# Softplus as exp and ln in small steps, and a new timetable for them, in a decoder layer on one core

## The reference, cut to what matters

```python
hidden = _rmsnorm(residual, norm_w)
x, z = jnp.split(hidden @ W_in, 2, axis=-1)          # 1024 channels each
x = silu(causal_conv(x, conv_w, 4 taps) + conv_b)
x_dbl = x @ W_x                                      # 64 + 16 + 16 columns
dt = jax.nn.softplus(x_dbl[..., :DT_RANK] @ W_dt + b_dt)
Bm, Cm = x_dbl[..., 64:80], x_dbl[..., 80:]
A = -jnp.exp(A_log)
def step(h, inp):                                    # over the 224 rows
    x_t, dt_t, B_t, C_t = inp
    dA = jnp.exp(dt_t[..., None] * A)
    h = dA * h + (dt_t * x_t)[..., None] * B_t[:, None, :]
    return h, jnp.einsum('bdn,bn->bd', h, C_t)
y = (scan(step) + x * D) * silu(z)
out = residual + y @ W_out
```

## Time and profile before

| | |
|---|---|
| median of 3 runs | 3411.76 us (3411.43 to 3412.63) |
| the profiled execution's own time | 3412.63 us |
| its span, first to last instruction | 3411.2 us |
| PE, DVE, ACT, POOL busy over the span | 92%, 75%, 66%, 51% |
| first scan to last scan of the first phase | 83 to 1867 us |
| ACT table loads in the program | 97, of 1283 ns each |

### The profile page before, as it was taken

The page is one execution under the profiler, slowest core; times in us unless marked ns, Lnnn a source line. Parts: engine busy times, 40 slices in busy tenths (PEclk is TensorE's granted clock), DMA queues, the critical chain, the costliest instruction groups (busy, mean ns, idle before and its releaser), DMA issues. The chain is left out here.

```text
span 3411.2 us, 59151 instructions
## 1 busy us (share of the span) xinstructions
PE 3150.7 (92%) x20736; PEld 2194.3 (64%) x20736; DVE 2573.8 (75%) x4542; ACT 2262.6 (66%) x5049; POOL 1741.6 (51%) x1195
## 2 busy tenths in 40 slices
PE   5699899999999989999998899999999999899999
PEld 4567566665666656665665566666666666578887
DVE  1899999999999999999977577777777777523232
ACT  4678777777778777777764577777777777622222
POOL 1677888788887888788885000100000000055554
PEclk8899999999999999999999899999999999999999
DMA  6667667676777667667665121211211221210100
GB/s 180 167 182 191 182 173 189 180 192 179 175 184 186 184 166 189 187 180 185 173 172 175 54 73 54 89 50 48 84 59 48 75 69 61 65 59 25 47 28 25
DMA packets 286293, 424.98 MB, mean 125 GB/s; under 512 B 28753, under 2 KB 226129, under 8 KB 281394
## 3 DMA queue, kind: packets, MB, share of 16 engines
q1 hardware_dynamic: 278637, 411.44, 44.0%
q10 hardware_dynamic: 7365, 9.77, 1.0%
HBM read 320.12 MB, written 101.02 MB: 123 GB/s over the span
## 5 line engine op out<-in xcount | busy, mean ns | idle before, releaser
L772 POOL TENSOR_TENSOR a_hs<-a_rep,a_bmat 128x896 f32<-128x896 f32 x512 | 1061.4, 2096 | 323.7 <-PE a_yps L319 321.5
L439 ACT ACTIVATE a_states<-a_rep,a_a_neg 128x224 f32<-128x224 f32 x2048 | 795.7, 439 | 205.7 <-DVE a_hs L675 198.0
L668 DVE TENSOR_TENSOR_SCAN a_states<-a_states,a_hs 128x900 f32<-128x900 f32 x384 | 778.9, 2028 | 97.4 <-ACT a_states L439 95.0
L1381 DVE CUSTOM_DVE_ANT_0 b_sc<-sps,early_mask 112x375 f32<-112x375 f32 x1024 | 499.6, 544 | 134.6 <-PE sps L1127 128.7
L1268 ACT ACTIVATE b_sc<-b_sc,b_nmax 112x750 f32<-112x750 f32 x512 | 467.2, 913 | 0.7 <-DVE b_nmax L1387 0.7
L1141 PEld LDWEIGHTS b_tps<-ident,b_sc 112*125 112x125 f32 x3072 | 358.1, 189 | 168.8 <-issue 118.4
L341 PE MATMUL a_work<-early_scan_hT,w_in 128*128 128x224 f32 x2048 | 433.3, 370 | 13.5 <-issue 9.8
L341 PEld LDWEIGHTS a_work<-early_scan_hT,w_in 128*128 128x128 f32 x2048 | 411.8, 202 | 39.4 <-issue 29.2
L1141 PE MATMUL b_tps<-ident,b_sc 112*125 112x112 f32 x3072 | 405.3, 281 | 26.0 <-DVE b_pT L1395 18.8
L675 DVE TENSOR_TENSOR a_hs<-a_states,a_cmat 128x896 f32<-128x896 f32 x384 | 419.0, 1091 | 13.2
L1521 POOL TENSOR_SCALAR b_x_var<-mv 112x2 f32<-112x2 f32 x16 | 3.4, 214 | 814.8 <-DVE mv L1432 814.8
(11 more groups left out here) (189 smaller groups left out, 4735.5 us busy)
## 6 DMA issues: line engine op xcount, KB each, us to landing
a_rep<-du_scratch SPq DMA_DIRECT2D x512, 224.0 KB, 5.5
w_in<-W_in_dram SPq DMA_DIRECT2D x128, 512.0 KB, 4.4
du_scratch<-early_du SPq DMA_DIRECT2D x16, 1792.0 KB, 6.3
ctx<-ctxT_dram SPq DMA_DIRECT2D x48, 500.0 KB, 5.8
v_scratch<-kv_out SPq DMA_DIRECT2D x96, 250.0 KB
k_scratch<-kv_out SPq DMA_DIRECT2D x96, 250.0 KB, 4.4
b_keys<-k_scratch SPq DMA_DIRECT2D x8, 1500.0 KB, 9.6
b_v<-v_scratch SPq DMA_DIRECT2D x8, 1500.0 KB
```

What stands on the lines that cost most here:

```text
L439: e = act.activation(rows(states[:, g % DA, :])[:, q, 1:ROW], rep[tile % REPS][:, j, 0, :], ACT.Exp, scale=a_neg[:, g % SLOTS, q:q + 1])
L668: dve.tensor_tensor_scan(state if g % G4 else whole, state, whole, 0.0, ALU.mult, ALU.add).then_inc(S["scan"], 1)
L772: pool.tensor_tensor(hs[g % RING][:, :, 1:ROW], rep[tile % REPS][:, j, 1, :].unsqueeze(1).broadcast_to([P, Q, L]), bmat[b % 2][:], ALU.mul ...
L1381: dve.tensor_tensor_reduce(out=sc[buffer_of(block)][:, j, cols], in0=sps[0:TT, j, 0:HALF], in1=mask[:, block % 2, cols], scale=-1.0, scala ...
```

## The change

Softplus is no longer one activation but max(x, 0) + ln(1 + exp(-|x|)), pair by pair. ScalarE (`softplus_parts`): Abs into the buffer "conv", Relu into "dt", Exp, and a Square with a bias, written back to the PSUM bank. VectorE (`softplus_series`): two operations on it that make the first terms of a series for small arguments, the second added into dt. ScalarE (`softplus_log`): Ln and a Relu with a bias, in "conv". GpSimd (`softplus_sum`): dt + conv for the whole batch, 128 x 1792, ahead of the product u. The bank is now free when VectorE's second operation is done. All functions are in the table set of the exponentials, so the loads around the softplus go (97 become 66). The next batch's last tap waits for the sum, since "conv" is in use until then.

The timetable changes with it. For `LATER`, in slots of the batch that is scanned: dt from 18, 18, 21, 21 to 6, 8, 10, 12; parts in 7, 9, 11, 13, series in 8, 10, 12, 14, logs in 9, 11, 13, 15, the sum in 18; silu of z from 25 to 20, u from 26 to 20, its store from 24 to 21, z one slot earlier. Three units of keys and values per batch move by a slot or two; in the last batch but one two move from slots 6 and 8, one from 29, to 18, 19 and 20.

```diff
-            "x_dbl": [-33], "xd": [-32], "store_bc": [-32], "dt": [-18, -18, -15, -15],
-            "softplus": [-15, -15, -15, -15], "skip": [-20, -19], "spread": [-19], "silu_z": [-11], "u": [-10],
+            "x_dbl": [-33], "xd": [-32], "store_bc": [-32], "dt": spaced(-30, 2), "parts": spaced(-29, 2),
+            "series": spaced(-28, 2), "logs": spaced(-27, 2), "skip": [-20, -19], "spread": [-19], "dt_sum": [-18],
...
             def dt_raw(b, pair):
-                bank = take_bank(("dt", b, pair), "dt", PAIRS * b + pair + 1)
+                bank = take_bank(("dt", b, pair), "part", PAIRS * b + pair + 1)
...
                 if b:
-                    act.wait_ge(S["xs"], 2 * b)
+                    act.wait_ge(S["dt"], b)
...
-                act.preload_act_table_set("natural_log_exp_and_others" if b else "softplus")
+                act.preload_act_table_set("natural_log_exp_and_others")
...
-            def softplus(b, pair):
-                act.wait_ge(S["dt_ps"], PAIRS * b + pair + 1)
+            def softplus_parts(b, pair):
+                n = PAIRS * b + pair
+                cols = slice(2 * pair, 2 * pair + 2)
+                view = pair_of_tiles("dt", b, pair)
+                act.wait_ge(S["dt_ps"], n + 1)
                 act.wait_ge(S["xs"], 2 * (b + 1))
-                act.activation(dt[:, 2 * pair:2 * pair + 2, :], pair_of_tiles("dt", b, pair),
-                               ACT.Softplus).then_inc(S["dt"], 1)
-                if pair == PAIRS - 1:
-                    act.preload_act_table_set("natural_log_exp_and_others")
+                steps.after(act.activation(conv[:, cols, :], view, ACT.Abs))
+                steps.after(act.activation(dt[:, cols, :], view, ACT.Relu))
+                steps.settle()
+                steps.after(act.activation(conv[:, cols, :], conv[:, cols, :], ACT.Exp, scale=-1.0))
+                steps.settle()
+                act.activation(view, conv[:, cols, :], ACT.Square, scale=3.0 ** -0.5,
+                               bias=series_bias[:]).then_inc(S["square"], 1)
+
+            def softplus_log(b, pair):
+                n = PAIRS * b + pair
+                cols = slice(2 * pair, 2 * pair + 2)
+                act.wait_ge(S["part"], n + 1)
+                steps.after(act.activation(conv[:, cols, :], conv[:, cols, :], ACT.Ln, bias=1.0))
+                steps.settle()
+                act.activation(conv[:, cols, :], conv[:, cols, :], ACT.Relu, bias=log_small[:]).then_inc(S["log_part"], 1)
...
+            def softplus_series(b, pair):
+                cols = slice(2 * pair, 2 * pair + 2)
+                series = pair_of_tiles("dt", b, pair)
+                dve.wait_ge(S["square"], PAIRS * b + pair + 1)
+                steps.after(dve.scalar_tensor_tensor(out=series, in0=series, scalar=13.0 / 16.0, in1=conv[:, cols, :],
+                                                     op0=ALU.add, op1=ALU.mult))
+                steps.settle()
+                dve.scalar_tensor_tensor(
+                    out=dt[:, cols, :], in0=series, scalar=LOG1P_SMALL * (LOG1P_SMALL ** 2 / 3 - LOG1P_SMALL / 2 + 1),
+                    in1=dt[:, cols, :], op0=ALU.min, op1=ALU.add).then_inc(S["part"], 1)
...
+            def softplus_sum(b):
+                pool.wait_ge(S["part"], PAIRS * (b + 1))
+                pool.wait_ge(S["log_part"], PAIRS * (b + 1))
+                pool.tensor_tensor(dt, dt, conv[:], ALU.add).then_inc(S["dt"], 1)
```

More of the change, by code:

```diff
@@ L16 @@
 NEG_INF_SCALE = -1e9
+LOG1P_SMALL = 2.0 ** -8
 class Memory:
@@ L231, in mamba_phase @@
         n_weights = 11
-        n_const = 4
+        n_const = 6
         def spaced(first, step):
@@ L619, in scalar_program @@
                     keep_xd(b)
-                for b, pair in due(slot, "softplus"):
-                    softplus(b, pair)
+                for b, pair in due(slot, "parts"):
+                    softplus_parts(b, pair)
+                for b, pair in due(slot, "logs"):
+                    softplus_log(b, pair)
                 for b, _ in due(slot, "silu_z"):
@@ L728, in vector_program @@
                     dve.tensor_scalar(a_neg[:], a_neg[:], -1.0, None, ALU.mult).then_inc(S["const"], 1)
+                    dve.wait_ge(S["log_small"], 1)
+                    steps.after(dve.tensor_scalar(log_small[:], log_small[:], -1.0, None, ALU.mult))
+                    steps.settle()
                 for b, pair in due(slot, "older_taps"):
                     older_taps(b, pair)
+                for b, pair in due(slot, "series"):
+                    softplus_series(b, pair)
                 for b in range(B):
@@ L815, in gpsimd_program @@
                     gains(b)
+                for b, _ in due(slot, "dt_sum"):
+                    softplus_sum(b)
                 for b, _ in due(slot, "u"):
```

38 lines of the change are left out of this document (22 added, 16 removed).

## The result

The changed kernel takes 3470.35 us (3466.92 to 3472.16, 4 runs), the kernel before 3411.6 beside it (4 runs): ratio 1.0171, 95% interval [1.0153, 1.0188], slower by 58.7 us where 27 were forecast, 0.35 us beyond the upper end of the range. The profiled execution took 3465.96 us (span 3464.6), 53.3 more than that of before.

What follows compares the result with a forecast made beforehand. VectorE, 93% busy, was taken to set the 110.2 us batch period. 78.6 - 52 - 3.8 + 2.5 + 2 = +27.3 us on 3412.63 gave 3439.9, 3439 us for the median; range 3402 to 3470.

Steps and rivals of the forecast that it cites:

- The series: VectorE's eight added operations per batch, 0.68 us each, between scans with nothing to hide them: +78.6 us (70 to 104).
- Before batch 2: Places ahead of the thirteen batches: batch 1's softplus wait -3.8 us, GpSimd's sum and product +2.5, later first scan +2.
- ScalarE's work: ScalarE's added activations, net +8.8 us per batch, said to fit in 26 us of idle time and costed at nothing.
- Waits that go and come: Scan waits in the thirteen batches: 2.3 of 6.3 us per batch left, 4.0 saved, -52 us (0 to -82).
- The late last pair of dt: TensorE's last dt pair, behind an output projection and tile sum: a new wait of 0.7 us per batch (0 to 1.7).
- The silu of z: ScalarE's burst behind a tap, in a step with a short scan: about 1.1 us of wait per batch.
- for places that I don't see: Allowance for waits at unforeseen meeting places in a batch: 0.5 us per batch.
- GpSimd becomes late: Rival: sum and product, 3.99 us each, delay step 21's input; 1.5 us per batch, +22 us, 3462 us; chance 0.12.
- TensorE's lateness goes too: dt and 4.4 us of TensorE losses per batch leave the crowded half; worth some 1.0 us of the remaining waits.
- the 4.88 us group: TensorE group after the last two dt pairs, 4.88 us where its like takes 3.19; forecast to disappear.
- ScalarE overflows: Rival: exponentials late at each of four pairs, about 1 us each, 1.7 at the last; +83 us, 3495 us; chance 0.12.
- The table loads: Two loads per batch around ScalarE's softplus go; 1.30 us a switch by the row, 2.6 us per batch freed.

Runs made afterwards that it cites:

- e1: Changed kernel with VectorE's two series operations on one column of each tile: 3445.89 us, ratio 1.0103.
- e4: Changed kernel with ScalarE's Abs, Exp, Ln and last Relu on one column, GpSimd adding dt to itself: 3411.78 us, ratio 1.0002.
- e13: Changed kernel with only Ln and the last Relu on one column, GpSimd adding dt to itself: 3426.27 us, ratio 1.004.
- e14: Changed kernel with GpSimd's sum on one column, all else whole: 3439.74 us, ratio 1.0085.
- e6: Changed kernel with GpSimd's product u and its store two slots later, in 22 and 23: 3446.44 us, ratio 1.01.
- e3: Kernel before with one Relu in place of Softplus and no table loads around it: 3394.99 us, ratio 0.9955.
- e5: Changed kernel with the last pair of dt in slot 11, ahead of the first output projection: 3475.94 us, ratio 1.0187.

## Why the prediction was wrong

- **The series** (78.6 us forecast). Means 0.616 and 0.625 us, inside the bounds of 0.61 and 0.88 and under the 0.68 taken: 15 x 4.8 = 72. That nothing hides it was half wrong: e1 got only half of it back, because ScalarE is as full in the same slots.
- **Before batch 2** (11.2 us forecast from the terms: 2 ahead of the loop, two series, -3.8, +2.5). Measured 8.0; first scan 84.59, forecast near 85. Right.
- **ScalarE's work** ("so I cost the added activations at nothing"). The sum itself was right: parts 2.17 us and logs 1.17 in the timeline, forecast 2.12 and 1.21, and no scan of slots 9 to 13 waits. But the cost at nothing is the step that failed. It was asked only whether the exponentials of the next slot come in time. The last logarithm has another reader, GpSimd's sum, that waits 1.8 us for it (23.4 us over the thirteen batches), and GpSimd's own four microseconds of sum were costed at nothing in these batches too. e4 and e13 get back 58 and 44 us by lightening ScalarE, of which 0.8 us per batch of GpSimd are not ScalarE's; e14 gets back 31 with ScalarE's work whole.
- **Waits that go and come** (saved 4.0 per batch forecast, -52 us). Saved were 6.4 - 4.5 - 0.8 = 1.1 by the waits, and 4.8 - 3.4 = 1.4 by the period. The late last pair of dt came, at twice the 0.7 taken but inside its 0 to 1.7: slot 15 has the 0.70, and the series in slot 14 waits 0.8 more. The silu of z is at 0.67, forecast 1.1, but only because the scan ahead of it has already waited: where slot 21 does not wait (e4, e6, e14), slot 22 has 1.3 to 1.7. The 0.5 "for places that I don't see" were 2.9: slots 1, 4, 21, 29, all gone in e14. The thirteen batches missed by 43.9 - 16.1 = 28 us: the 2.4 us more at such places are 31, other waits some 3, and the series was 6 cheaper. e14 gives back the same 31.
- **"GpSimd becomes late"** was a rival at 1.5 us per batch, 3462 us. Its mechanism came true, with 0.96 us at slot 21; with what follows behind it, it is worth 24 (e6) to 31 us (e14). Its 3462 was already the forecast's sum with 22 on top, 27 + 22 = 49; but it stood as another case at a chance of 0.12, and so entered the forecast's own time at nothing, though nothing in the forecast excludes it.
- **"TensorE's lateness goes too"** failed with it: the wait for the softplus and the 4.88 us group went, but a stop of 3.04 us with a slow restart came in slot 20, at the head of the full stretch. There it costs 4.8 us in the batch shown, as much as the 4.4 us that were to leave. The new waits for the series ahead of the output projection, 3.47 us in one batch, were foreseen.
- **"ScalarE overflows"**: its price of 1 us at each pair did not come; with VectorE lighter (e1) waits of 0.50 and 1.87 us stand at two of the pairs.
- **The table loads**: 31 fewer, worth 16 us in the old timetable (e3). The row gave 1.30 us a switch; 2 x 1.30 x 15 = 39 us of ScalarE, of which less than half was on the path.

## What to carry to other kernels

When an engine gets more work that "fits", list every reader of its last result, and not only the engine that bounds the kernel: more than half of what a lighter ScalarE gets back (2.2 of 3.7 us per batch in e4) stood behind the full slots, by way of GpSimd and TensorE. Relieving GpSimd is worth 24 to 31 us though the scan that waits for GpSimd loses only 13, since TensorE stops there too, just ahead of its fullest stretch. A rival that can happen together with the forecast belongs into its sum, at its chance. And where two engines are equally full, lightening one brings half, and a wait removed (e5) may only move to the next engine in the chain.
